# First attention: context of group 3 moved next to that of group 4, denominators ahead of context 2

## The reference, cut to what matters

```python
q, k, v = tanh(x @ Wq + bq), tanh(x @ Wk + bk), tanh(x @ Wv + bv)   # x: (4, 1024, 128)
alpha = einsum('bhqd,bhkd->bhqk', q, k) / 8                          # causal
ctx = einsum('bhqk,bhkd->bhqd', softmax(alpha), v)
x = x + layernorm(tanh(ctx @ Wo + bo))
```

## Time and profile before

| | us |
|---|---|
| median of 3 runs | 1631.6 (1628.72 to 1643.32) |
| the profiled execution | 1633.24 |
| its span, first to last instruction | 1631.4 |
| PE busy | 1551.1 (95%) |
| DVE busy | 1419.4 (87%) |
| ACT busy | 1227.8 (75%) |
| POOL busy | 461.1 (28%) |

### The profile page before, as it was taken

One profiled execution on the slowest core, in us unless ns is written; L12 is line 12 of the kernel. 1 busy time (PEld: TensorE's weight loads), 2 busy tenths in 40 slices (PEclk: granted clock), 3 DMA queues, 4 the chain that ended last, 5 costly groups with the idle time before them and its releaser, 6 DMA issues.

```text
span 1631.4 us, 38607 instructions
## 1 busy us (share of the span) xinstructions
PE 1551.1 (95%) x14806; PEld 701.8 (43%) x14806; DVE 1419.4 (87%) x2102; ACT 1227.8 (75%) x1698; POOL 461.1 (28%) x563
## 2 busy tenths in 40 slices
PE   7899999999999999998899999999999999989996
PEld 4344444444444444445333333333333333466774
DVE  6777778888888888998899999999999999397888
ACT  4667666677666676664798999899989999666776
POOL 3311112222333323334135242324332432120004
PEclk9999999999999999999999999999999999899998
DMA  5311001111011110001112000200030000000001
GB/s 146 73 39 40 30 30 40 39 37 39 21 39 39 37 39 34 26 3 33 34 41 53 15 14 15 53 14 15 19 82 19 15 28 2 1 8 8 14 14 52
DMA packets 46606, 52.98 MB, mean 32 GB/s; under 512 B 9279, under 2 KB 33551, under 8 KB 46482
## 3 DMA queue, kind: packets, MB, share of 16 engines
q1 hardware_dynamic: 45584, 50.05, 10.5%
q10 hardware_dynamic: 898, 1.22, 0.3%
HBM read 15.07 MB, written 10.49 MB: 16 GB/s over the span
## 4 chain that ended last, share of the span: by engine, by line
PE 63%; DVE 22%; ACT 10%; issue 3%; POOL 1%; ACTq 0%; POOLq 0%; DVEq 0%
DVE arena L2408 16%; PE psum L590 15%; PE psum L571 12%; ACT arena L2164 7%; PE psum L1916 5%; PE psum L533 5%; PE psum L1547 5%; PE psum L1514 4%; PE psum L608 3%; PE psum L1927 3%; PE psum L628 3%; PE psum L1902 1%; PE psum L553 1%; PE psum L554 1%; PE psum L555 1%
## 5 line engine op out<-in xcount | busy, mean ns | idle before, releaser
L2408 DVE TENSOR_REDUCE arena<-psum 128x2 f32<-128x1024 f32 x490 | 565.7, 1214 | 11.1 <-PE psum L1927 9.8
L2164 ACT ACTIVATE arena<-psum 128x512 f32<-128x512 f32 x980 | 519.6, 600 | 52.0 <-PE psum L1902 46.1
L755 ACT ACTIVATE arena<-psum 128x2048 f32<-128x2048 f32 (+1 forms) x160 | 274.0, 1713 | 229.0 <-PE psum L571 228.9
L1916 PE MATMUL psum<-arena 128*32 128x256 f32 x4096 | 329.2, 393 | 1.4 <-ACT arena L2184 0.2
L859 POOL TENSOR_SCALAR_AFFINE_SELECT arena<-arena 128x512 f32<-128x512 f32 (+1 forms) x160 | 152.7, 972 | 508.7 <-ACT arena L755 508.7
L590 PE MATMUL psum<-arena,hs 128*64 128x512 f32 (+3 forms) x1536 | 283.0, 496 | 0.2 <-POOL arena L859 0.2
L1902 PE MATMUL psum<-arena 32*128 32x512 bf16 x1024 | 255.9, 385 | 1.3 <-ACT arena L2164 0.4
L571 PE MATMUL psum<-arena 64*128 64x512 f16 (+3 forms) x2304 | 215.0, 324 | 2.1 <-DVE arena L907 1.6
L1927 PE MATMUL psum<-arena 32*128 32x512 bf16 x980 | 189.9, 384 | 21.0 <-DVE arena L2408 13.1
L907 DVE TENSOR_TENSOR arena<-arena 128x1024 f16<-128x1024 f32 x64 | 78.4, 1226 | 101.4 <-ACT arena L734 101.4
L590 PEld LDWEIGHTS psum<-arena,hs 128*64 128x64 f32 x1536 | 95.9, 136 | 141.5 <-issue 125.2
(11 more groups left out here) (222 smaller groups left out, 2160.1 us busy)
## 6 DMA issues: line engine op xcount, KB each, us to landing
arena<-arena SPq DMA_DIRECT2D x30, 512.0 KB, 2.9
arena<-arena SPq DMA_DIRECT2D x46, 128.0 KB, 2.2
arena<-latent_q SPq DMA_DIRECT2D x64, 64.0 KB, 2.0
arena<-latent_k SPq DMA_DIRECT2D x64, 64.0 KB, 2.0
arena<-arena SPq DMA_DIRECT2D x60, 64.0 KB, 2.2
X<-in_L_attn_states SPq DMA_DIRECT2D x4, 512.0 KB, 4.4
latent_q<-arena SPq DMA_DIRECT2D x16, 96.0 KB, 2.3
latent_k<-arena SPq DMA_DIRECT2D x16, 96.0 KB, 2.3
```

Of the source, the lines that this page charges most:

```text
L755: nc.scalar.activation(probs[g], SC[:, :, 0:WIDTH[g]], ACT.Exp, scale=DH ** -0.5).then_inc(exp_done, 1)
L1916: last = nc.tensor.matmul(OT[ROWS * c:ROWS * (c + 1), h * HALF // 2:(h + 1) * HALF // 2], v_cols[par][:, kt, 2 * pr + i, :], e_probs[u % 4 ...
L2164: nc.scalar.activation(e_probs[u % 4][:, i * HALF:(i + 1) * HALF], ring(n, u, i), ACT.Exp, scale=KD ** -0.5).then_inc(e_done, 1)
L2408: nc.vector.tensor_reduce(half_tops[:, kh, qt, 2 * pr:2 * pr + 2], src.rearrange("p (i c) -> p i c", i=2), AX.X, ALU.max).then_inc(top_don ...
```

## The change

PE's order within a pair is changed; nothing is added or removed, no wait is changed, and no other engine's program is touched. Context 3 leaves its place behind scores 4 and runs in the next pair, behind that pair's scores 0 and directly ahead of context 4. Denominators and context 2 change places. Behind the last pair, context 3 of it runs ahead of its context 4.

```diff
             def pair(i, par, last=False, norm=False):
                 if at_least(i, 1):
+                    context(i - 1, 3, 1 - par)
                     context(i - 1, 4, 1 - par)
                 if last:
                     turn_first_states()
...
                 context(i, 1, par)
                 scores(i, 3, par)
-                context(i, 2, par)
                 if at_least(i, 1):
                     denominators(i - 1, 1 - par)
                 else:
                     pe.wait_ge(tanh_done, 8)
                     turn_normal(pe, 1, PJ)
+                context(i, 2, par)
                 scores(i, 4, par)
-                context(i, 3, par)
                 if at_least(i, 2):
                     output(i - 2, par)
...
             each_pair(pe, pair)
+            context(N1 - 1, 3, 1)
             context(N1 - 1, 4, 1)
```

## The result

| | before | after |
|---|---|---|
| median, us | 1632.95 (20 runs, 1628.13 to 1643.32) | 1649.58 (20 runs, 1638.88 to 1658.5) |
| ratio to before | | 1.0096, 95% interval 1.0079 to 1.0113 |
| the profiled execution | 1633.24, mean clock 0.991 | 1638.93, mean clock 0.995 |
| its span | 1631.4 | 1637.1 |

The changed kernel is 0.96% slower (13 to 18 us by the interval); 10.3 us were forecast, and a range up to 1650.

What follows compares the result with a forecast made beforehand. PE was taken to bound the first attention. Norm pairs +11.1, pairs without norm -1.2, behind pair 1 +0.4, last pair 0: +10.3 on the median of 1631.6, giving 1641.9, 0.63% slower; range 1630 to 1650.

Steps and rivals of the forecast that it cites:

- The values' wait for the addition to `acc`: Norm pairs: values wait for DVE's L920; the move of context 3 removes it, a gain of 0.1, counted as 0.14.
- The hold of output: Norm pairs: with context 3 gone, output waits 0.84 for DVE's L927, making the period 0.53 longer.
- The term of that way: Way from DVE to PE, end of L927 to start of output: taken as 0.10, between readings of 0.05 and 0.14.
- Denominators first: Denominators ahead of context 2 wait for the second tanh, with 0.85 to spare: cost nothing.
- Rival C: Transposes keep 1.57: norm pairs held 0.27 longer, pairs without norm 0.16; 1648.9, chance 0.15.
- The ends: First and last pairs: +0.4 behind pair 1, nothing behind pair 0, 0 in the last pair.
- the last pair's term: PE idles 1.4 ahead of denominators, but DVE's chain closes the stage: 0, bounds -0.5 to +1.4.
- rival F: PE's clock falls for its idles; half the clock in one pair of ten costs some 60 us; chance 0.02.
- rival A: Likeliest case: output held in norm pairs alone; 1641.9, between 1635 and 1647; chance 0.60.
- B: Not slower: output is not held, every pair saves its border; -6.9, 1624.7; chance 0.10.
- D: Nothing: a wait of 0.3 instead of 0.84, for instance L974 taking 2.45; 1631 to 1634; chance 0.08.
- rival E: Idle before output takes over its border, saving 0.15 a second time in 21 norm pairs; 1638.7; chance 0.05.

## Why the prediction was right

- **What was expected to be saved.** Contexts 3 and 4 in one block: 2.74, forecast 2.73. Period without norm 22.13, forecast 22.15. The values' wait for the addition to `acc` is gone.
- **The hold of output.** Counted as the forecast counts it, from the start of scores 4 plus 0.76 (596.35) to output (597.14), it is 0.79, forecast 0.84. The idle of 0.73 in the row counts from the modelled end of scores 4. The term of that way, 0.10, was too large: L928 ends at 597.09 and output starts at 597.14, 0.05, the lower of the two readings. Over 21 pairs this is 1 us. Period 22.93, forecast 22.97. In pairs 28 and 29 it is 23.05, against 22.56 before.
- **Why DVE is late.** The prediction followed L927 back to scores 2, 9.76 earlier. In the changed kernel it is the same: scores 2 end at 587.32, L928 at 597.09, 9.77. The run that shortened only this stretch gave back 15.7.
- **Denominators first.** Cost nothing in the loop, and they removed the wait between the two transposes in pairs without norm, as said (1.31 for 1.57). Rival C falls with that.
- **The ends.** Values behind pair 1 start at 81.67 in place of 81.15. From the first wait on, which came 0.93 earlier, that is +1.45, and without the 0.79 of clock +0.7; forecast +0.4. The last pair was taken at 0 with a bound of +1.4; with PE idle for 1.71, the kernels that differ only there differ by 1.3, and from its scores 3 to the addition the full change takes some 1.6 more (38.33, from 752.10, against 37.74 less 1.06 of clock). So the ends cost +2.3 where +0.4 was forecast: the last pair's term was mis-sized, by about its bound.
- **The sum.** Forecast +10.3; 11.0 at whole clock behind the first attention, 10.0 to 11.1 between whole runs of one clock. The 21 norm pairs cost 10.1 where 11.1 was forecast, and the ends made up for it: that the total comes so close is in part luck.
- **Where it fell short.** The forecast set the clock aside (rival F) because a busy share of 80% had kept 1.00. For the norm pairs that was right: 1.00 from 80 to 740 us in each of the ten traces. But the prediction took one execution's sum to the median as if the clock were a constant, while runs of one kernel range from 0.984 to 0.995 (before) and from 0.981 to 0.995 (after), 14 and 20 us. So the measured median is 16.6 above before, not 10.3: some 3 us go with a lower mean clock, and the rest is where the middle run of so wide a spread happens to lie. Whether the longer idle behind pair 0 carries part of the 3 us stays open, and with 27 runs they may be chance.
- **Luck in the range.** The median, 1649.58, is 0.4 inside the range and above the 1635 to 1647 given for rival A alone. The upper end, 1650, was set by rival C, which did not come about. So the mechanism and its size at one clock were right, and that the range still held the median is luck. Rivals B and D fall with the hold of 0.79; L975, which was to be quicker in D, takes 2.79.
- **The rule weighed (rival E).** Contexts 3 and 4 have no border between them and output its usual 1.45 (597.14 to 598.59) although PE had idled 0.73 before. So E falls: the 0.15 did not come a second time. The Trainium skill (TensorEngine Tiling (Array Packing), Key Properties) says that changing the tiling mode drains the engine; whether the cost at a border is that drain, no run here shows.

## What to carry to other kernels

Work that covers a wait must be counted before it is moved: context 3 looked like filler that could stand anywhere, but it hid about 0.8 us of DVE's lateness 21 times, while bringing it next to its like saved 0.15. When a wait appears, follow the engine that ends it back to where it was released last, and look for work in that stretch that nobody is waiting for; moving 0.54 us of moments there turned a loss of 10 us into a gain of nearly 6 (1623.2 against 1628.9), and of 7 with the ends kept as well. Compare runs at equal clock before putting a difference of medians down to the program.

## What the runs showed of the hardware

- Two equal additions on DVE take 2.48 when POOL's mask starts behind the start of the second, and 2.79 when it starts ahead of it (594.15, where the second starts at 594.33). The second alone grows from 1.22 to 1.53. The two masks one by one in the changed kernel, and the first one with later moments:

```profile
594.15 0.63 POOL L860 TENSOR_SCALAR_AFFINE_SELECT arena<-arena 128x512 f32<-128x512 f32 x1 [13.79 <-ACT arena L756]
594.75 1.38 POOL L860 TENSOR_SCALAR_AFFINE_SELECT arena<-arena 128x256 f32<-128x256 f32 x1
```

```profile
606.16 1.25 POOL L860 TENSOR_SCALAR_AFFINE_SELECT arena<-arena 128x512 f32<-128x512 f32 x1 [13.97 <-ACT arena L756]
```

The Trainium skill (SBUF — State Buffer, Who interferes with whom) says that a DVE instruction with two SBUF inputs contends with a POOL instruction that reads SBUF, and that the order of issue decides which of them blocks. The traces agree: the addition that starts behind the first mask loses 0.31, of the 0.45 that were left of that mask (594.78 - 594.33), and a mask that starts behind an addition ends only after it. The second mask above, half as long as the first, takes 1.38 and ends at 596.13, 0.27 behind the addition; the 1.25 one ends at 607.41, 0.50 behind it (605.69 + 1.22 = 606.91). Spans on POOL are rough, so whether the block is a full one in both directions is not measured to 0.1 us.
- The clock of PE fell to its lower level in different stretches in different runs of the same program. In the ten traces these lie between 20 and 80 us, 770 and 810, 1390 and 1470, and behind 1610, and never in 270 to 740, whether PE was busy for 467.42 of these 470 us or for 454.27.
